# A GNN and mixture-of-experts kernel: the lower part of one operand is computed behind the routing on VectorE, not ahead of it

## The reference

```
x = x + gnn(layernorm(x))     # h = x @ W.T + b, summed over edges, weighted by 1/sqrt(degree)
z = layernorm(x)
base   = z @ base_W.T + base_b
shared = (z @ shared_A.T) @ shared_B.T                 # rank 16
gate   = softmax(z @ router_W.T + router_b)            # 6 experts, the top 2 are kept
w      = top-2 gates / (their sum + 1e-6)
routed = sum over experts e of w[e] * (z @ routed_A[e].T) @ routed_B[e].T
out    = x + base + shared + routed
```

## Time and profile before

| | us |
|---|---|
| median of 3 runs | 2072.52 |
| lowest and highest run | 2072.22, 2073.84 |
| the profiled execution | 2073.73 |
| its span from first to last instruction | 2072.0 |
| PE busy in the span | 1947.6 (94%) |
| DVE busy in the span | 1472.4 (71%) |
| ACT busy in the span | 907.9 (44%) |
| POOL busy in the span | 934.1 (45%) |

### The profile page before, as it was taken

The page is one execution under the profiler, slowest core; times in us unless marked ns, Lnnn a source line. Parts: engine busy times, 40 slices in busy tenths (PEclk is TensorE's granted clock), DMA queues, the critical chain, the costliest instruction groups (busy, mean ns, idle before and its releaser), DMA issues.

```text
span 2072.0 us, 31600 instructions
## 1 busy us (share of the span) xinstructions
PE 1947.6 (94%) x9583; PEld 1611.7 (78%) x9583; DVE 1472.4 (71%) x3525; ACT 907.9 (44%) x1533; POOL 934.1 (45%) x954
## 2 busy tenths in 40 slices
PE   7999999999999999943999999999999999999999
PEld 6778777777777878733788878788887888888887
DVE  6877887887876666753677767776776767676775
ACT  4455555555555555532333333333333334343342
POOL 1712444444424500015455565555555655555550
PEclk9999999999999999976999999999999999999999
DMA  6633454454443443473233333333333333333311
GB/s 242 209 112 139 174 184 159 172 191 154 170 150 132 150 155 124 157 247 96 63 97 92 100 92 101 102 102 83 99 91 93 95 100 101 100 84 92 101 58 62
DMA packets 148959, 260.20 MB, mean 126 GB/s; under 512 B 56077, under 2 KB 75357, under 8 KB 148822
## 3 DMA queue, kind: packets, MB, share of 16 engines
q1 hardware_dynamic: 99478, 237.85, 31.9%
q0 software_dynamic: 49344, 20.85, 8.0%
HBM read 273.80 MB, written 129.74 MB: 195 GB/s over the span
## 4 chain that ended last, share of the span: by engine, by line
issue 39%; PE 24%; POOL 21%; DVE 10%; ACT 3%; DMA 2%; POOLq 0%; DVEq 0%; SPq 0%; ACTq 0%
POOL acc L830 8%; PE bo L1491 5%; PE bo L1493 4%; PE bo L1495 4%; POOL piece L799 3%; POOL counted L766 2%; POOL counts L780 2%; POOL xpw L708 2%; POOL pw L901 2%; POOL slots L787 2%; DVE acc L2123 1%; DVE xn L1817 1%; PE bt L1541 1%; PE bo L1340 1%; POOL tick_pool L683 1%
## 5 line engine op out<-in xcount | busy, mean ns | idle before, releaser
L830 POOL DMA_INDIRECT acc<-h_rows,row_now x312 | 503.5, 1614 | 110.1 <-issue 110.0
L1351 PE MATMUL bo<-wr_hi,left_hi 128*128 128x512 f32 x1008 | 403.1, 400 | 16.4 <-issue 9.8
L1355 PE MATMUL bo<-wr_hi,left_lo 128*128 128x512 f32 x1008 | 394.5, 391 | 0.0
L1353 PE MATMUL bo<-wr_lo,left_hi 128*128 128x512 f32 x1008 | 394.1, 391 | 0.0
L708 POOL TENSOR_TENSOR xpw<-xpin,neg_half 128x1 f32<-128x1 f32 x79 | 72.7, 921 | 503.1 <-DVE xpin L1659 503.1
L1491 PE MATMUL bo<-wr_hi,sum_hi 128*128 128x512 f32 x624 | 248.2, 398 | 5.6 <-DVE acc L2123 4.1
L1493 PE MATMUL bo<-wr_lo,sum_hi 128*128 128x512 f32 x624 | 244.4, 392 | 0.0
L1495 PE MATMUL bo<-wr_hi,sum_lo 128*128 128x512 f32 x624 | 244.1, 391 | 0.0
L1351 PEld LDWEIGHTS bo<-wr_hi,left_hi 128*128 128x128 f32 x1008 | 190.2, 189 | 66.1 <-issue 29.7
L1355 PEld LDWEIGHTS bo<-wr_hi,left_lo 128*128 128x128 f32 x1008 | 190.0, 189 | 40.4
L1353 PEld LDWEIGHTS bo<-wr_lo,left_hi 128*128 128x128 f32 x1008 | 190.6, 189 | 36.5
(11 more groups left out here) (229 smaller groups left out, 4301.5 us busy)
## 6 DMA issues: line engine op xcount, KB each, us to landing
xn<-x SPq DMA_DIRECT2D x79, 512.0 KB
r_rows<-xn SPq DMA_DIRECT2D x79, 512.0 KB, 2.7
acc<-r_rows SPq DMA_DIRECT2D x79, 512.0 KB, 4.2
out<-acc SPq DMA_DIRECT2D x79, 512.0 KB, 3.1
h_rows<-hrow SPq DMA_DIRECT2D x144, 256.0 KB
acc<-h_rows,row_now POOLq DMA_INDIRECT x312
wr_raw<-w_t SPq DMA_DIRECT2D x16, 256.0 KB, 6.5
piece<-base_t SPq DMA_DIRECT2D x64, 64.0 KB, 4.2
```

Source lines behind the costliest of these rows:

```text
L830: nc.gpsimd.indirect_dma_start(to[:], None, h_dram, bass.IndirectOffsetOnAxis(ap=at, axis=0), bounds_check=NPAD - 1, oob_is_err=False, com ...
L1351: nc.tensor.matmul(ps, left_hi[n][:, k, :], wr_hi[n][:, k, :], start=False, stop=False, skip_group_check=True)
L1353: nc.tensor.matmul(ps, left_hi[n][:, k, :], wr_lo[n][:, k, :], start=False, stop=False, skip_group_check=True)
L1355: last = nc.tensor.matmul(ps, left_lo[n][:, k, :], wr_hi[n][:, k, :], start=False, stop=(k == 3), skip_group_check=True)
```

## The change

In VectorE's step the call that makes the lower part of S4 stands first, ahead of the weighed sum C12A, the routing and the low-rank values. The change puts it behind them, directly ahead of the weighed sum C22A. Nothing is added or removed, and the other engines' programs stay as they are.

```diff
@@ def step(s), block vector
                 if not s.has(0):
                     return
-                y_low(p, S4, ys4[:])
                 weighed_sum(s.acc(0, 0), s.tile(0, 0), 1, second_bank[:],
                             (y_done, y_product_at(p, S2)))
                 choose(p, 2)
                 hidden(p, 2)
+                y_low(p, S4, ys4[:])
                 weighed_sum(s.acc(0, 1), s.tile(0, 1), 1, third_bank[q][:],
                             (y_done, y_product_at(p, S1)))
                 if s.has(1):
```

## The result

The changed kernel takes 2081.0 us (median of 8 runs, 2077.11 to 2083.84) against 2073.1 us (8 runs, 2071.6 to 2075.32). The ratio is 1.0036, with a 95% interval of 1.0026 to 1.0047: slower by 7.5 us (7.9 between the medians), where 1.6 us were forecast, too little to be told from no change. Two runs further down, one of e3 (2199.71 us) and one of e7 (5167.09 us), fell in a slow state and are left out of every median and ratio. The profiled execution took 2081.72 us.

A forecast was written before the change was run, and what follows sets the result against it. TensorE was taken to bound the second phase. Ordinary steps 0, seven branch steps 1.05 and last step 0.52 summed to 1.6 us, giving 2074.1 us from the median 2072.52, range 2071.5 to 2078.

The forecast's parts named there:

- What bounds the kernel: Second phase: TensorE bounds it, busy 1008.32 of 1020 us, waiting for VectorE in only 7 of 37 steps.
- The ordinary step, cost 0: Thirty steps: C12A 0.30 us earlier, C22A and all behind it 0.31 us later, absorbed by the margins; cost 0.
- The seven steps, cost 1.05 us: Steps where the counted loop branches back: one more register instruction behind the stall, 7 x 0.15 us; bounds 0 and 4.3 us.
- What TensorE gains at S3 it waits for at S4: Seven steps: S3 starts earlier, but S4 needs C22A and its lower part behind the same sum of work; no gain.
- longer by 0.5 to 0.7 us: Expected trace sign in the seven steps: TensorE's wait at S4 grows this much, the one at S3 shrinks by about 0.5.
- The last step, cost 0.52 us: Last step: C12A cannot move up, C22A ends 0.61 us later, S4 starts at 2058.98 instead of 2058.46; cost 0.52 us.
- the whole shift lands on the margins: Rival: C12A or the routing does not move up in ordinary steps, so 0.61 us eats the margins; 2079.4 us, chance 0.05.
- GpSimd does not hold up the moved instruction: Denies a rival: moved `y_low` waits for GpSimd's indirect DMA to end, 45 us in all; 2119 us, chance 0.03.
- A gain at S3: Rival: in the seven steps S3's shorter wait is really won, up to 0.61 us each; 2068.7 us, chance 0.04.

The follow-up runs named there:

- e3: Changed kernel plus three spare TensorE matmuls between the low-rank transposes and product S4, in the first step of each loop turn: 2075.2 us.
- e7: Kernel before, old order, with S4's lower part computed once more ahead of C22A in each loop turn's first step: 2083.65 us against 2073.36.
- e5: Kernel before with only VectorE's part of the second phase written out in full, other engines keeping their loop: 2054.48 us against 2073.36.
- e2: Kernel before with the move made in 31 steps, all but the first of each loop turn: 2073.78 us against 2072.88, ratio 1.0001.
- e1: Kernel before with the move made only in the first step of each loop turn (8 of 39 steps): 2081.6 us against 2072.88.
- e4: Kernel before with S4's lower part put directly behind C12A, ahead of the routing, in all steps: 2083.25 us against 2072.88.

## Why the prediction was wrong

**What bounds the kernel** was right: TensorE waited in seven steps only, and e5 shows that VectorE's branch is the cause of all seven.

**The ordinary step, cost 0:** right, and close in its numbers. In the changed kernel, on VectorE and then on TensorE:

```profile
1530.85 0.75 DVE L2123 SCALAR_TENSOR_TENSOR acc<-acc,dis,bo 128x512 f32<-128x512 f32 x1 [1.22 <-PE bo L1495]
...
1535.58 0.68 DVE L2114 TENSOR_TENSOR sum_lo<-ys,sum_hi 128x512 fp32r<-128x512 f32 x1
1536.18 0.74 DVE L2123 SCALAR_TENSOR_TENSOR acc<-acc,dis,bo 128x512 f32<-128x512 f32 x1
...
1539.37 0.42 DVE L2106 TENSOR_TENSOR hs_lo<-bo,hs_hi 113x256 fp32r<-113x256 f32 x1
```

```profile
1530.42 0.39 PE L1495 MATMUL bo<-wr_hi,sum_lo 128*128 128x512 f32 x1
...
1537.36 0.48 PE L1491 MATMUL bo<-wr_hi,sum_hi 128*128 128x512 f32 x1
...
1540.19 0.39 PE L1531 MATMUL bo<-bl_hi,hs_hi 113*128 113x512 f32 x1
```

S2 ends at 1530.42 + 0.39 = 1530.81 and C12A starts at 1530.85, 0.04 behind it (0.05 was taken). C22A ends at 1536.92, 0.44 us ahead of S4 (0.41 forecast); `hidden_low` ends at 1539.79, 0.40 ahead of the low-rank product (0.39). e2 measured the cost as 0 within its interval (0.9992 to 1.0010).

**The seven steps, cost 1.05 us: this step of the prediction failed.** On VectorE in the changed kernel:

```profile
1336.24 0.75 DVE L2123 SCALAR_TENSOR_TENSOR acc<-acc,dis,bo 128x512 f32<-128x512 f32 x1 [1.65 <-issue]
...
1340.98 0.68 DVE L2114 TENSOR_TENSOR sum_lo<-ys,sum_hi 128x512 fp32r<-128x512 f32 x1
1341.58 0.74 DVE L2123 SCALAR_TENSOR_TENSOR acc<-acc,dis,bo 128x512 f32<-128x512 f32 x1
```

The second gap behind the branch stands ahead of C12A now, as forecast. VectorE's waits of the kind "issue" (total, times, longest), first in the kernel before from 1040 to 2060 us, then in the changed kernel from 1040 to 2068 us:

```profile
DVE acc L2132 <- issue: 17.0, 7, 2.7
DVE sum_lo L2114 <- issue: 10.6, 7, 1.9
```

```profile
DVE acc L2123 <- issue: 11.5, 7, 2.0
```

The second gap grew by 0.9 us in seven steps. The shift of S4 was right too: it starts 1342.38 - 1333.03 = 9.35 us behind the transposes that follow S2 (L1517), against 1342.55 - 1333.27 = 9.28 us before; over the seven steps this adds up to 0.7 us, where 1.05 was taken. What failed is the sentence "What TensorE gains at S3 it waits for at S4", which was costed at zero. The exchange leaves the sum of TensorE's idle time much as it was, but not its place: a piece of idle time that stood alone ahead of S3 was put beside another one ahead of S4. The prediction even forecast this wait, "longer by 0.5 to 0.7 us" (it grew from 0.18 to 0.78), and read the clock of 1.00 as given, where it was a thing that the change could lose. Behind the pair the clock fell to 0.50 in five of the seven steps, and 7.2 us followed, so that the seven steps cost 7.9 us in place of 1.05. With the last step's 0.6 (below) that makes 8.5 us, against 8.0 us between the two profiled executions; the changed kernel reached the first pair's S4 0.3 us earlier (1012.27 against 1012.54 us).

The Trainium skill has a rule that would have been a rival: "TensorE: Matmul & The Clock Gate", section "A second HAM failure mode: psum-queue depth-cycling", tells of a kernel in which short idle times between groups of matmuls let the clock swing between its levels and cost throughput. The trace agrees, with five falls behind waits of 1.04 to 1.14 and 0.78 us.

**The last step, cost 0.52 us:** right. On VectorE

```profile
2060.25 0.75 DVE L2123 SCALAR_TENSOR_TENSOR acc<-acc,dis,bo 128x512 f32<-128x512 f32 x1 [4.19 <-PE bo L1495]
```

and on TensorE:

```profile
2066.47 0.47 PE L1491 MATMUL bo<-wr_hi,sum_hi 128*128 128x512 f32 x1 [0.35 <-DVE acc L2123]
```

S4 starts 2066.47 - 2060.25 = 6.22 us behind C12A's start, against 2058.46 - 2052.83 = 5.63 before: 0.59 us later. It is the wait of 0.35 us in the table above.

**The rivals.** That the whole shift lands on the margins gave 2079.4, near the measured time, but for a cause that did not occur: TensorE waits for VectorE in no ordinary step (its nine waits for a weighed sum are the seven and one behind the branch and that of the last step). GpSimd does not hold up the moved instruction, which takes 0.68 us at 1535.58, wholly inside an indirect DMA of GpSimd:

```profile
1535.43 1.58 POOL L830 DMA_INDIRECT acc<-h_rows,row_now  x1 [1.20 <-issue]
```

A gain at S3 was not given back. None of them was the mechanism.

**What stays open.** Not every such pair of waits makes the clock fall. In the last of the seven steps of the changed kernel the waits are the same and the pace holds:

```profile
1903.03 0.47 PE L1525 MATMUL bo<-ident,hs 128*113 128x128 f32 x2 [1.07 <-DVE hs L2098]
1904.28 0.50 PE L1491 MATMUL bo<-wr_hi,sum_hi 128*128 128x512 f32 x1 [0.78 <-DVE acc L2123]
...
1907.24 0.47 PE L1531 MATMUL bo<-bl_hi,hs_hi 113*128 113x512 f32 x1
```

The first step behind a branch behaves likewise. The trace has a hint at what decides. The five falls begin at 1342.70, 1455.34, 1567.98, 1680.62 and 1793.26 us, each 112.64 us behind the one before, although the S4s beside them are 112.2 to 112.8 us apart. They come 0.32 to 1.23 us behind S4's start; the same spacing carried on would have put one 1.28 us ahead of S4's start in the first of the seven steps and one 1.62 us behind it in the last, and there the clock held. e1, e4 and e7 show the same spacing (once doubled, where a step was left out): the 22 falls of the four traces begin from 0.11 us ahead of S4's start to 1.23 us behind it, and in the six steps without one it would have lain outside. So it seems to depend on when the waits come, and not on the waits alone, whether the clock falls; then five falls and not three or seven were luck. No run shifted the waits in time by itself, so this was not shown.

Nor does the profile of one execution tell how many falls the others had. Their mean granted clock speaks for a number that varies: it is 0.976 to 0.979 in the eight runs of the changed kernel, one stretch of 3.4 us at half clock is worth 3.4 / 2 / 2080 = 0.0008 of it, and the two runs at 0.979 are among the three fastest. But the kernel before spreads by 6 us over the 21 runs beside e1 to e4, nearly as much as the changed kernel's 6.7 us over eight, with its clock at 0.980 to 0.982. What makes up that spread stays open.

## What to carry to other kernels

When a change moves a wait of a busy TensorE to another place, the sum of its idle time is not the whole price: look at what it is put beside, and allow for the granted clock to fall behind a cluster of waits, after which the matmuls that follow take nearly twice their time for a while. Read the clock in the same short windows as the waits, before and after. And where waits recur once per turn of a counted loop, look for the engine that comes late out of the branch; writing out that engine's loop alone was worth 19 us here, and made the order of its work indifferent.

## What the runs showed of the hardware

- The granted clock fell to 0.50 for 3.4 us around the start of a product behind two waits of about 1.05 and 0.78 us, or 1.70 and 0.18, with two small transposes between them, although TensorE had waited for nothing in the whole step before in the changed kernel. It did so in 22 of 28 such places (5 of 7 in the changed kernel, 6 in e1, 6 in e4, 5 in e7), and in none of the seven of the kernel before, with waits of 1.02 to 1.28 and 0.18 us. Each fall cost 1.3 to 1.5 us.
- A loop's branch on VectorE made it late by two gaps in each turn, one ahead of its first instruction (17.0 us in seven turns of the kernel before) and one behind that instruction (10.6 us in seven). Written out in full, the same engine's program showed no such gap; TensorE's steps over the branches had been 18.8 us too long, and 18.9 us went.
- Three spare matmuls in the wait of 0.78 us, in one step of each turn, took 5.8 us off the changed kernel (2081.0 to 2075.2 us); the clock stayed up in all ten runs (0.981 to 0.983).
- A subtract of VectorE on 128x512 values in SBUF took 0.68 us wholly inside an indirect DMA instruction of GpSimd of 1.58 us, and 0.69 us at its old place inside one of 1.56 us.
